# Masks of a running maximum made on ScalarE as distances, in the second layer of a graph network kernel

## The reference, cut to what matters

```
xr = jnp.einsum('nd,rdf->rnf', x, W)          # 3 relations
qi = xr[etype, dst] @ q
kj = xr[etype, src] @ k
alpha = jax.nn.leaky_relu(qi + kj, NEG_SLOPE)
m = jax.ops.segment_max(alpha, dst, num_segments=n_nodes)
e = jnp.exp(alpha - m[dst])
z = jax.ops.segment_sum(e, dst, num_segments=n_nodes)
a = e / (z[dst] + EPS)
msg = (a[:, :, None] * oj.reshape(-1, heads, out_ch)).reshape(-1, heads * out_ch)
out = jax.ops.segment_sum(msg, dst, num_segments=n_nodes)
```

## Time and profile before

| what | us |
|---|---|
| time, median of 3 runs | 1641.3 (1640.31 to 1646.14) |
| span of the profiled execution | 1756.8 |
| PE busy | 1503.4 (86%) |
| DVE busy | 928.3 (53%) |
| POOL busy | 1032.8 (59%) |
| ACT busy | 220.5 (13%) |
| line 975, both layers, 166 instructions | 137.2 |
| line 960, both layers, 332 instructions | 81.7 |
| line 980, both layers, 166 instructions | 136.9 |

### The profile page before, as it was taken

How to read it: one execution, slowest core, us unless ns; L and a number is a source line. 1 busy time by engine, 2 the same in 40 slices (tenths; PEclk the granted TensorE clock), 3 DMA queues, 4 the chain that set the end, 5 groups by cost and what they waited for, 6 DMA issues and landing times.

```text
span 1756.8 us, 24768 instructions
## 1 busy us (share of the span) xinstructions
PE 1503.4 (86%) x6326; PEld 879.5 (50%) x6330; DVE 928.3 (53%) x2169; ACT 220.5 (13%) x530; POOL 1032.8 (59%) x1112
## 2 busy tenths in 40 slices
PE   5889989899856998878889899954997999898986
PEld 2445545455534555545544455533554655454543
DVE  8575722343433888996777787702533345222233
ACT  1555200000000111000100023320110011000000
POOL 1598266665443778884077776514656662666664
PEclk9989999999965999878999999965998999999998
DMA  8201588888620131101188877730232111888888
GB/s 300 100 19 48 173 272 258 272 291 273 227 66 4 54 109 38 37 20 37 58 268 262 265 248 252 208 100 1 56 84 54 47 46 46 270 263 273 261 262 265
DMA packets 86808, 271.76 MB, mean 155 GB/s; under 512 B 32156, under 2 KB 32531, under 8 KB 86743
## 3 DMA queue, kind: packets, MB, share of 16 engines
q0 software_dynamic: 51072, 199.44, 37.5%
q1 hardware_dynamic: 34807, 65.62, 10.5%
q10 hardware_dynamic: 864, 5.90, 0.9%
HBM read 239.28 MB, written 31.62 MB: 154 GB/s over the span
## 4 chain that ended last, share of the span: by engine, by line
PE 65%; issue 11%; POOL 9%; DMA 7%; DVE 4%; another core or an unknown queue 1%; ACT 1%; DVEq 0%; POOLq 0%; SPq 0%; PEldq 0%; ACTq 0%
PE ps L1271 13%; PE ps L1310 13%; PE ps L1244 10%; POOL ring L506 7%; PE ps L1312 6%; PE ps L1313 6%; PE ps L1142 5%; DMA ring<-keys,idxr 4%; PE ps L1188 3%; PE ps L1185 2%; PE ps L1205 2%; PE ps L1092 2%; PE ps L1063 1%; DMA ring<-rows,idxr 1%
## 5 line engine op out<-in xcount | busy, mean ns | idle before, releaser
L1271 PE MATMUL ps<-wreg,hT 128*128 128x384 f32 x1440 | 490.5, 503 | 8.2 <-PEq L1264 6.6
L506 POOL DMA_INDIRECT ring<-keys,idxr x312 | 330.7, 1060 | 190.3 <-issue 82.8
L475 POOL DMA_INDIRECT ring<-rows,idxr x304 | 312.8, 1029 | 218.1 <-PEq L1299 76.5
L1271 PEld LDWEIGHTS ps<-wreg,hT 128*128 128x128 f32 x1440 | 282.7, 197 | 204.9 <-issue 27.8
L1310 PE MATMUL ps<-ring,zw 128*128 x664 | 227.5, 496 | 25.8 <-DVE zw L1040 19.2
L1244 PE MATMUL ps<-ring,zw 128*128 x664 | 224.6, 495 | 24.7 <-DVE zw L869 19.5
L975 DVE TENSOR_TENSOR hn<-hn,al 128x1024 f32 (+1 forms) x166 | 137.2, 827 | 166.4 <-POOL al L524 108.3
L475 POOL DMA_INDIRECT ring<-rows,idx x152 | 148.1, 975 | 116.2 <-PE ps L1244 58.9
L1310 PEld LDWEIGHTS ps<-ring,zw 128*128 128x128 f32 x664 | 122.8, 191 | 124.9 <-issue 52.8
L1244 PEld LDWEIGHTS ps<-ring,zw 128*128 128x128 f32 x664 | 125.3, 192 | 118.5 <-issue 40.7
L1038 DVE TENSOR_TENSOR ring<-ring,al x166 | 159.3, 960 | 35.3 <-SPq L393 19.6
(11 more groups left out here) (185 smaller groups left out, 1246.8 us busy)
## 6 DMA issues: line engine op xcount, KB each, us to landing
wreg<-in_L_gnn_W SPq DMA_DIRECT2D x11, 2304.0 KB, 9.1
rows<-stage SPq DMA_DIRECT2D x30, 386.0 KB
rows<-stage SPq DMA_DIRECT2D x30, 384.5 KB
stT<-targets_row ACTq DMA_DIRECT2D x6, 960.0 KB
ring<-keys,idxr POOLq DMA_INDIRECT x312
ring<-rows,idxr POOLq DMA_INDIRECT x304
rows<-stT SPq DMA_DIRECT2D x10, 384.0 KB, 3.0
xs<-in_x SPq DMA_DIRECT2D x3, 1152.0 KB, 13.1
```

Of the source, the lines that this page charges most:

```text
L475: nc.gpsimd.indirect_dma_start(ring[:, t % (2 * RING), 0:WIDTH[l]], None, rows[l], bass.IndirectOffsetOnAxis(idx[:, t:t + 1], 0)).then_inc ...
L506: nc.gpsimd.indirect_dma_start(kb[:, n % KSEMS, t % KB, 0:4], None, keys[l], bass.IndirectOffsetOnAxis(idxr[:, t:t + 1], 0)).then_inc(k_in ...
L1271: last = mm(ps[:, 2 * (nt % 2) + h, 0:HALF], hT[:, k, nt * P:(nt + 1) * P], wreg[:, r % 2, k, h * HALF:(h + 1) * HALF], start=(k == 0), st ...
```

## The change

In layer 1 the two masks of each pair are no longer made by DVE. ACT makes them as `Abs(column * 2^120 - target * 2^120)`: 0 in the target's column, at least 2^120 in any other. DVE subtracts that from the score instead of adding `negm`. A new array `tlb` holds the targets times -2^120 (one DVE instruction on 128x180, when the slots are set up). A new semaphore `scored_in` counts DVE's subtractions: ACT's masks of pair i wait until the subtraction of pair i-2 is done, because the two share a buffer, and DVE's maximum waits on it for its own pair's subtraction.

The place of the masks in ACT's queue is fixed: two pairs ahead of the first half, then behind half h all pairs up to `MASKS_AT[h] = 76 * (h + 1) // 55 + 2` (3 behind half 0, 25 behind 15, 37 behind 25, 78 behind 54), that is one or two pairs behind each half, and behind half 55 a loop over the pairs from 78 on, whose end is known at run time only. ACT also reads the bounds into registers ahead of layer 1. Layer 2 is as before.

```
+ACT_MASKS = (1,)
+BIG = 2.0 ** 120
+SURE_PAIRS = (E + PAIR - 1) // PAIR
+LAST_PAIRS_AT = 2 * (R * NT - 3) + 1
+MASKS_AT = [(SURE_PAIRS - 3) * (h + 1) // LAST_PAIRS_AT + 2 for h in range(LAST_PAIRS_AT)]
...
+            pairs = load_bounds(act)[NT]
+            def distances(l, i, bias_at):
+                if not isinstance(i, int) or i >= 2:
+                    act.wait_ge(scored_in[l], i - 1)
+                for b in range(2):
+                    nc.scalar.activation(negm[...], iota_f[:, 0:P], ACT.Abs, bias=bias_at(b), scale=BIG).then_inc(nm_step[l], 1)
+            def sure_distances(l, first, end):
+                for i in range(first, end):
+                    distances(l, i, lambda b: tlb[:, 2 * i + b:2 * i + b + 1])
...
+                if l in ACT_MASKS:
+                    act.wait_ge(wq2_done, R)
+                    sure_distances(l, 0, 2)
...
+                            n = 2 * (r * NT + nt) + h
+                            if l in ACT_MASKS and n < LAST_PAIRS_AT:
+                                sure_distances(l, MASKS_AT[n - 1] if n else 2, MASKS_AT[n])
+                            if l in ACT_MASKS and n == LAST_PAIRS_AT:
+                                with act.Fori(SURE_PAIRS - 1, pairs) as i:
+                                    distances(l, i, lambda b: tlb_bytes[:, ds(i * 8 + 4 * b, 4)].bitcast(F32))
...
+            V.tensor_scalar(tlb[:, :], tl[:, :], -BIG, None, ALU.mult)
...
-                for b in range(2):
+                for b in range(2 if l not in ACT_MASKS else 0):
                     V.tensor_scalar(negm[:, 0, b, :], iota_f[:, 0:P], tl[:, b:b + 1], NEG, ALU.not_equal, ALU.mult).then_inc(nm_step[l], 1)
...
+                        if l in ACT_MASKS:
+                            dve.wait_ge(m_chain[l], i + (2 * j + 3))
+                            V.tensor_tensor(scored[...], scores_at(i, 0, H, 2)[...], negm[...], ALU.subtract).then_inc(scored_in[l], 1)
+                            dve.wait_ge(scored_in[l], i + 1)
+                            V.tensor_tensor(run, run, scored[:, :, 0:H, :], ALU.max).then_inc(m_chain[l], 1)
```

More of the change, by code:

```diff
@@ L201, in gnn_kernel @@
         tl = sb("tl", [P, T])
+        tlb = sb("tlb", [P, T])
         idx0 = sb("idx0", [P, T], I32)
@@ L291, in gnn_kernel @@
         nm_step = {l: sem(f"nm_step{l}") for l in (1, 2)}
+        scored_in = {l: sem(f"scored_in{l}") for l in (1, 2)}
         m_chain = {l: sem(f"m_chain{l}") for l in (1, 2)}
@@ L316, in gnn_kernel @@
         tl_bytes = tl[:, :].bitcast(U8)
+        tlb_bytes = tlb[:, :].bitcast(U8)
         def row_at(i, b, first, end):
@@ L635, in _ @@
             act.wait_ge(rstd_ready, 2)
+            pairs = load_bounds(act)[NT]
[3 more added lines that the diff above has]
+                for b in range(2):
+                    nc.scalar.activation(negm[:, i % 2, b, :] if isinstance(i, int) else negm[:, ds(i % 2, 1), b, :].rearrange("p a c -> p (a c)"), iota_f[:, 0:P], ACT.Abs, bias=bias_at(b), scale=BIG).then_inc(nm_step[l], 1)
+            def sure_distances(l, first, end):
+                for i in range(first, end):
+                    distances(l, i, lambda b: tlb[:, 2 * i + b:2 * i + b + 1])
             for l in (1, 2):
                 H = HEADS[l]
+                if l in ACT_MASKS:
+                    act.wait_ge(wq2_done, R)
+                    sure_distances(l, 0, 2)
                 for r in range(R):
@@ L973, in _ @@
                         dve.wait_ge(nm_step[l], 2 * i + 2)
[L974 to L981, removed]
+                        if l in ACT_MASKS:
+                            dve.wait_ge(m_chain[l], i + (2 * j + 3))
+                            V.tensor_tensor(scored[:, :, 0:H, :], scores_at(i, 0, H, 2).rearrange("p (b h) -> p b h", b=2).unsqueeze(3).to_broadcast([P, 2, H, P]),
+                                            negm[:, ds(i % 2, 1), :, :].rearrange("p a b c -> p (a b) c").unsqueeze(2).to_broadcast([P, 2, H, P]), ALU.subtract).then_inc(scored_in[l], 1)
+                            dve.wait_ge(scored_in[l], i + 1)
+                            V.tensor_tensor(run, run, scored[:, :, 0:H, :], ALU.max).then_inc(m_chain[l], 1)
+                        else:
+                            dve.wait_ge(m_chain[l], 2 * i + (2 * j + 3))
+                            V.tensor_tensor(scored[:, :, 0:H, :], negm[:, ds(i % 2, 1), :, :].rearrange("p a b c -> p (a b) c").unsqueeze(2).to_broadcast([P, 2, H, P]),
+                                            scores_at(i, 0, H, 2).rearrange("p (b h) -> p b h", b=2).unsqueeze(3).to_broadcast([P, 2, H, P]), ALU.add).then_inc(m_chain[l], 1)
+                            for b in range(2):
+                                mask(i + 1, b)
+                            dve.wait_ge(m_chain[l], 2 * i + (2 * j + 4))
+                            V.tensor_tensor(run, run, scored[:, :, 0:H, :], ALU.max).then_inc(m_chain[l], 1)
+                    dve.wait_ge(m_chain[l], (1 if l in ACT_MASKS else 2) * bnd[j + 1] + (2 * j + 3))
                     dve.sem_inc(z_in[l], 1)
```

1 line of the change is left out of this document (added).

## The result

The changed kernel takes 1625.3 us (median of 4 runs, 1620.3 to 1627.4) where the kernel before takes 1640.8 (4 runs, 1634.8 to 1646.1). The ratio is 0.9902, with a 95% interval from 0.9879 to 0.9926: 15.5 us or 1.0% faster. The prediction said 1639, in a range from 1633 to 1646, so the time lies outside it, on the fast side. Rival 1 (PE's wait and its clock loss vanish, 1633.5) was nearest, and it too was 8 us short.

A forecast was written before the change was run, and what follows sets the result against it. PE, busy 86% of the span, was taken as the bound, so DVE counts only where PE waits for it. From gains of 0.9 to 9 us it took 2.3: 1641.3 - 2.3 = 1639, range 1633 to 1646.

The forecast's parts named there:

- Rival 1: Layer 1: POOL's gathers catch the gap everywhere, PE's wait and clock loss vanish; -6.5 to -9.2 us, 1633.5; chance 0.13.
- walking through twelve gathers: POOL in layer 1: two gathers per DVE pair, then score steps, give a batch of 19.2 or 18.2 us.
- two masks on ACT: ACT in layer 1: two activations per pair cost about 0.7 us, 58 us over 83 pairs, covered by idle time.
- ACT's line 682: Layer 1: a PE wait on this line would show the prediction wrong; ACT's halves were to have 1.5 us to spare.
- the same 1.23: DVE in layer 1: the subtracting instruction was costed at the adding one's 1.23 us.
- rival 3: POOL in layer 1: the gap is too short, one gather fits per pair; 1740 us and more; chance 0.03.
- step 1: DVE's pair in layer 1: a 0.16 us wait before the maximum makes it 2.83 instead of 2.97, saving 0.14 us.
- The lower end, 0.08: DVE's pair in layer 1: with a wait of 0.22 us the pair is 2.89 at worst, saving 0.08 us.
- the batches of 19.2 (missed) and 18.2 (caught): Layer 1: missing the gap leaves batches as before and gains 0.9 us in all; catching it gains up to 9 us.
- step 2: PE in layer 1: waits of 5.72 and 0.77 plus 2.7 us of clock cap the gain at 9.2 us.
- there is less to win: PE's wait in unprofiled runs: POOL's 0.30 us pauses are partly the profile's, so 2.3 us near the lower end was chosen.
- step 3: End of layer 1's maxima: tile 9's transposes come 1.9 us late at no cost, since scaled rows wait for gathered rows.

The follow-up runs named there:

- e7: The changed kernel with DVE's maximum in layer 1 taken over only one of each pair's two slots (128x512 instead of 128x1024): 1631.8 us, ratio 0.9956.
- e0_before: The kernel before, unchanged, run again for a second profile: 1638.5 us, with a profile span of 1636.7 us.
- e9: The kernel before with only PE's signal that the gathered rows' ring is free moved ahead of the projections in both layers: 1631.2 us, ratio 0.9956.
- e5: The changed kernel with PE's signal that the gathered rows' ring is free moved ahead of the projections in both layers: 1617.6 us, ratio 0.9849.
- e2: The changed kernel with two unused mask-size instructions put back on DVE between subtraction and maximum, ACT still making the masks: 1643.8 us, ratio 1.0028.
- e8: e7 with two unused mask-size instructions added on DVE between subtraction and maximum: 1621.8 us, ratio 0.9899.

## Why the prediction was wrong, point by point

**Right: what the change works on.** POOL's gathers and DVE's pairs move together, a gather needs a gap and then 0.8 us, and a batch follows by walking through twelve gathers. With the measured pair of 2.70 the same walk gives 5 x 2.70 + 1.26 + 1.23 + 0.81 + 1.6 = 18.4 for a batch whose second gather misses the gap, and 18.42 was measured. For one that catches it the first score step ends, as the prediction said, just behind DVE's last pair (5 x 2.70 + 2.49 = 16.0, and 0.1), and 1.3 more give 17.4; 17.5 was measured. In the changed kernel the batches are 18.42, 18.43 and 17.5 apart. Right too: two masks on ACT take 0.68 to 0.70 us (0.7 said); PE never waits for ACT's line 682 in the changed kernel; layer 2 stays as it was; the instruction that subtracts takes the same 1.23 as the one that added; rival 3, with its one gather per pair, didn't come, though e7 shows that it is a real mechanism.

**Wrong, step 1: the gap of 0.16 us.** The prediction took the distance between subtraction and maximum as 1.23 + 0.16 = 1.39, from a reduction that waits for a maximum. It is 1.26: the wait of a two-input instruction for one of the same form is 0.03 us. The pair was to be 2.83 and is 2.70, so the removal is worth 0.27 us a pair and not 0.14. The lower end, 0.08, was a bound from rows; the upper end had none. The nearest row was of another instruction, and the true lower bound of such a wait is zero, by which a pair is 2.67. From this term came the batches of 19.2 (missed) and 18.2 (caught), 18.4 and 17.5 in truth, so that even the worse case gains 0.75 us in each batch, where I had none. Six such batches are 4.5 us, and PE's wait ahead of tile 1 fell by 4.1.

**Wrong, step 2: the cap of 9.2 us.** "So all that PE could gain here" was read from the earlier trace rows, in an execution 115 us longer than the runs. In a profile of normal length PE waits for 13.4 us instead of 6.5, at four places instead of two, with two losses of clock instead of one (3.0 and 2.4 us). The ceiling, waits and clock together, was 18.8 us. I had seen that the profile was too long, and said so, but took the difference to lie in POOL's pauses of 0.30 us. They are 0.30 in every profile of the study. It lay, in this part, in the small matmuls of the spreads on PE, 12.4 against 8.4 us, and it worked the other way: with a quicker PE there are more and longer waits for DVE, not fewer. The remark "there is less to win" chose the low end, 2.3 us, for a reason that e0_before refutes.

**Wrong, step 3: the end of the maxima is covered.** The prediction said that tile 9's late transposes and the maxima's end weren't on the path, since the scaled rows wait for gathered rows, and "those depend on the projections' last rows". POOL's first gather depends on PE's signal too, and that comes behind the closing of the spread: [41.75 <-PEq L1299] names it in the kernel before. DVE's idle time of 6.35 us in the earlier trace rows was followed back one step, to the arrival of rows, and not the second, to what had let POOL begin. The first gather begins 10.6 us behind the end of the last projection before and 12.7 after the change; with the signal moved it is 3.9 (e9) and 3.8 (e5). So the rows alone would let POOL begin some 7 us sooner, and the 2.1 us that the change adds at tile 9 (a wait of 4.20 for 2.92, and slower transposes) are on the path, where the prediction had 1.9 us of lateness at a price of nothing. This error isn't what made the forecast too small, it works the other way: up to the end of the last projection the part is 15.4 us shorter (288.81 and 273.45), and 2.1 of them are lost behind it. Nor does the gain need the signal to reach the end. With the signal early in both kernels (e9 to e5) the stretch from the first projection to the first sum is 302.0 and 288.9 us, 13.1 less; with the signal where it was it is 307.4 and 294.0, 13.4 less.

**The size, then.** With the terms as measured, waits -5.5 and clock -4.6 make -10.1 us, more than the cap of 9.2 and four times the 2.3 that was forecast. The remainder of -3.2 lies in stretches without waits, and its largest piece came and went between two profiles of the changed kernel; the 4 us between the span's difference and the medians' are within what one execution differs from the next. Neither has a cause that these runs show.

## What to carry to other kernels

Hold the span of a profile against the run times before reading a cap from it. Here the profiled execution was stretched, two waits were hidden by it, and "all that could be gained" was read at half of what it was; where it can't be taken again, keep the range open on that side.

A wait taken from a row of another form of instruction is a guess, and its bound on the good side is zero. Follow the wait that you call a cover back through two steps, to whoever gives the signal: where a credit stands behind a wait that it doesn't need, moving it up was worth 7 us here, half of what the change brought.

## What the runs showed of the hardware that I had not expected

- Dependent two-input instructions of 128x1024 on DVE follow each other after 0.03 us (538.17 to 538.20), a reduction behind one after 0.14 to 0.16, and one with a register computation ahead after 0.22; one more wait on a register's value made that 0.30 (e2).
- A gather on POOL takes 0.94 to 0.96 us where it needn't wait, 1.13 to 1.22 where it waits a little for a gap, 2.00 where it misses one, and 1.86 in step with a pair of 2.17 us. The Trainium skill, page SBUF — State Buffer, section "Who interferes with whom", reports that `tensor_tensor` didn't stall a DMA's descriptor generation and gives an inferred reason for it. In e7 and e8 the same gathers take 1.86 and 0.94 us, and between the two kernels only DVE's instructions differ, so for these gathers as a whole that doesn't hold. The prediction said that the trace speaks against the inference itself. That was too strong: each of these gathers also reads its row numbers from SBUF (`idxr`), and the same section has DVE's two-input instructions contend with GpSimd instructions that read SBUF. No run here has a gather without that read, so which of its steps is held up stays open.
- A shorter instruction on DVE made the kernel slower (e7), and two useless ones made that kernel faster again (e8). The length of DVE's pair doesn't order the batches: pairs of 2.17, 2.52 and 2.70 us gave batches of 20.8, 16.75 and 18.4 us.
- In the twelve profiles of normal length, PE's waits for DVE ahead of transposes in layer 1 were followed by eight transposes in 1.91 to 1.94 us where the wait was 4.18 us or longer (thirteen, up to 11.04), and in 1.06 to 1.13 us where it was 3.50 or shorter.
